# Four instead of two score products per step in the last attention's maxima stage

## The reference

```python
scores = jnp.einsum('bhtk,bhsk->bhts', q, k) * scale
weights = jax.nn.softmax(scores, axis=-1)
out = jnp.einsum('bhts,bhsk->bhtk', weights, v)
```

## Time and profile before

| | us |
|---|---|
| median of 3 runs | 3852.59 |
| lowest, highest | 3845.99, 3853.17 |
| profiled execution, whole | 3852.74 |
| its span, first to last instruction | 3851.0 |

### The profile page before, as it was taken

How to read it: one execution, slowest core, us unless ns; L and a number is a source line. 1 busy time by engine, 2 the same in 40 slices (tenths; PEclk the granted TensorE clock), 3 DMA queues, 4 the chain that set the end, 5 groups by cost and what they waited for, 6 DMA issues and landing times.

```text
span 3851.0 us, 43741 instructions
## 1 busy us (share of the span) xinstructions
PE 3115.1 (81%) x16174; PEld 1567.3 (41%) x16174; DVE 2426.6 (63%) x4576; ACT 1662.7 (43%) x2458; POOL 596.6 (15%) x425
## 2 busy tenths in 40 slices
PE   3647868997699868997699968998699977996698
PEld 1124423553245433554245532554235532464145
DVE  4634876568756776568765776668755786634442
ACT  3504625465255634465154644446154643432231
POOL 2001000311023010321013010321013110211030
PEclk8568969998799979998699989998799988997696
DMA  3151175302842165402843047412753128412261
GB/s 112 27 95 58 46 123 139 113 14 77 145 144 68 28 106 154 124 22 60 152 133 88 20 104 121 151 39 50 136 133 102 32 81 136 137 58 65 57 203 45
DMA packets 331910, 355.91 MB, mean 92 GB/s; under 512 B 98529, under 2 KB 264225, under 8 KB 330081
## 3 DMA queue, kind: packets, MB, share of 16 engines
q1 hardware_dynamic: 331697, 353.11, 39.1%
HBM read 302.74 MB, written 49.66 MB: 92 GB/s over the span
## 4 chain that ended last, share of the span: by engine, by line
PE 52%; DVE 28%; DMA 7%; ACT 5%; issue 4%; POOL 2%; SPq 2%; ACTq 0%; DVEq 0%; POOLq 0%
DVE MX L1596 7%; PE PS L1805 6%; PE PS L1828 6%; PE PS L1832 5%; PE PS L1659 5%; PE PS L1667 5%; PE PS L1103 3%; DVE U L891 3%; PE PS L1773 3%; DVE U L898 3%; DMA UU<-k_scratch 3%; PE PS L1784 2%; DVE D L1650 2%; POOL D L1404 1%; DVE D L948 1%
## 5 line engine op out<-in xcount | busy, mean ns | idle before, releaser
L1404 POOL TENSOR_TENSOR D<-D,GW 128x512 f32<-128x512 f32 x320 | 434.7, 1359 | 1409.1 <-ACT D L1477 1173.6
L783 ACT ACTIVATE U<-U 128x2048 f32<-128x2048 f32 x256 | 488.0, 1909 | 184.3 <-DVE U L891 99.4
L1645 DVE SCALAR_TENSOR_TENSOR D<-D,PS 128x512 f32<-128x512 f32 x336 | 229.2, 682 | 399.2 <-ACT D L1481 283.6
L1477 ACT ACTIVATE D<-PS 128x512 f32<-128x512 f32 x336 | 200.2, 596 | 610.2 <-PE PS L1828 610.2
L1805 PEld LDWEIGHTS PS<-WST,D 128*128 128x128 f32 (+1 forms) x2688 | 353.0, 198 | 163.4 <-DVE D L1650 96.0
L1805 PE MATMUL PS<-WST,D 128*128 128x128 f32 (+1 forms) x2688 | 380.3, 286 | 29.3 <-DVE D L1650 29.2
L1832 PE MATMUL PS<-XT,WST 128*128 128x512 f32 (+1 forms) x672 | 372.6, 637 | 29.2 <-DVE D L1645 28.0
L898 DVE SCALAR_TENSOR_TENSOR U<-PP,RD,QB 128x512 f32<-128x512 f32 x512 | 364.1, 780 | 47.5 <-ACT QB L780 28.8
L1103 PE MATMUL PS<-U,resident 128*32 128x512 f32 x2048 | 304.6, 675 | 102.3 <-ACT U L783 102.3
L1828 PE MATMUL PS<-XT,WST 128*128 128x512 f32 (+1 forms) x672 | 369.6, 633 | 7.7 <-DMA WST<-in_pairs_dram 4.7
L1596 DVE TENSOR_REDUCE MX<-PS 128x2 f32<-128x1024 f32 x256 | 298.4, 1221 | 84.9 <-PE PS L1751 84.9
(11 more groups left out here) (345 smaller groups left out, 3907.2 us busy)
## 6 DMA issues: line engine op xcount, KB each, us to landing
GW<-gates_scratch SPq DMA_DIRECT2D x320, 256.0 KB, 4.3
WST<-in_pairs_dram SPq DMA_DIRECT2D x336, 192.0 KB, 2.4
U<-band_scratch SPq DMA_DIRECT2D x32, 1280.0 KB, 14.6
UU<-in_w_dram SPq DMA_DIRECT2D x64, 512.0 KB, 7.6
UU<-pad_scratch SPq DMA_DIRECT2D x8, 1792.0 KB
UU<-q_scratch SPq DMA_DIRECT2D x24, 384.0 KB
UU<-k_scratch SPq DMA_DIRECT2D x24, 384.0 KB
e_scratch<-D SPq DMA_DIRECT2D x8, 1024.0 KB, 4.5
```

The source lines that it names most:

```text
L783: e.activation(ring(i), ring(i), ACT.Gelu).then_inc(S["act"], 1)
L1404: e.tensor_tensor(AV[:, n % 3, :], AV[:, n % 3, :], GW[:, p // 2 % GWS, p % 2, :], ALU.mult).then_inc(S["gated"], 1)
```

## The change

In each of the 32 steps PE issues four products in place of two. The first two are the same product into the same bank, and the third and fourth likewise; each starts a new accumulation, so the second overwrites what the first wrote. The semaphore is raised by the fourth. Nothing else differs: the waits, the reductions and the results are the same.

```diff
-                for x in range(2):
+                for x in (0, 0, 1, 1):
                     last = e.matmul(PZ(j + x), QS3[:, hd, P * (j + x):P * (j + x) + P], KS3[:, hd, :], start=True, stop=True)
                 last.then_inc(S["s1_3"], 1)
```

## The result

The changed kernel takes 3875.4 us (median of 4 runs, 3872.86 to 3883.8) against 3852.9 us of the kernel before; the ratio is 1.0066, with a 95% interval of 1.0046 to 1.0086. Run once more beside other kernels it gave 3883.6 us and a ratio of 1.0068 (1.0055 to 1.0081). It is slower, by some 25 to 26 us by the two ratios; the medians alone differ by 22.5 and 29.2 us. One execution of inner (4978.7 us) and one of halves (5201.1 us) further down ran at a mean granted clock of 0.592 and 0.549 against 0.87 to 0.91 in all others, and are left out of the ratios.

What follows compares the result with a forecast made beforehand. The maxima stage was taken to be on the chain, paced by DVE at full clock and PE's bank loop at low. Terms 6.7 + 8.0 + 3.6 + 15.2 - 2.0 = 31.5 us on 3852.7 gave 3884 us, range 3870 to 3900.

Steps and rivals of the forecast that it cites:

- The stage ends what both threads wait for: Maxima stage: L1154 and L1162 sit in PE's queue behind its last step, so both threads go on from its end.
- The price of a product: PE, start to start: 0.42 us at 1.2 GHz and 0.22 us at 2.4 GHz, taken for repeated products too.
- Term 1: Ahead of the first reduction: two more low-clock products, not hidden, 0.84 us a stage, 6.7 us in eight stages.
- Terms 2 and 5: Stage start: slow low-clock steps cost 1.0 us a stage, 8.0 in all; the clock's rise gives 2.0 us back once.
- Term 3: Steps at full clock: the pace stays 1.18 us and never gets to 1.13; together 3.6 us.
- Term 4: Around L1154: products added on either side cost 0.79 us at each of 3 x 7 places; 15.2 us after 1.4 back.
- What makes the stage longer makes the turn longer: Maxima stage: on the chain nearly whole, so its growth passes to the turn; summed in full, 31.5 us.
- Rival 1: Clock does not rise in the stage or falls back; 171 us more, 4024 us; chance 3%.
- Rival 2: Denser PE carries full clock beyond the stage and into its start, speeding L1162; 3860.5 us; chance 3%.
- Rival 3: Repeated product nearly free at the full clock; 6.8 us stay, 3859.5 us; chance 3%.
- Rival 4: Half of the delay covered by a transfer or engine that ends after the stage anyway; 3868 us; chance 7%.
- The allowance of 10 us for the clock: Over seven turns, 10 us either way for where the clock falls and rises against the work.

Runs made afterwards that it cites:

- inner: Against the kernel before, repeated products only in steps 4 to 21, 24, 25, 28 and 29, away from the stage's start and L1154; ratio 1.0025.
- halves: Kernel before with each L1154 in two halves of 8 products, one step of the maxima really between them; ratio 0.9954.
- split: Kernel before with L1154 meant to be in two parts, but nothing came between them, so the queue is as before; ratio 1.0003.
- again: The changed kernel run once more without an edit, for a second profile; 3883.6 us, ratio 1.0068 to the kernel before.
- six: Each product three times instead of twice as in the change, six a step; ratio 1.0226 to the kernel before.
- first4: Against the kernel before, repeated products only in the first four steps of the stage; ratio 1.0017.
- beside: Against the kernel before, repeated products only in the six steps right beside the three L1154; ratio 1.0017.
- three: Against the kernel before, three products a step away from L1154 and two beside it; ratio 0.9993.
- warm7: Kernel before with seven products nobody reads while PE waits for the stacks ahead of the stage; ratio 0.9993.
- warm7_four: The changed kernel with seven products nobody reads while PE waits for the stacks; ratio 1.0054 to the kernel before.

## Why the prediction was right, and where it was off

The direction was right and the time lies in the range: 3875.4 us measured, 3884 forecast. Step by step:

- The stage ends what both threads wait for: right. The six turns with both threads grew from 440.5 to (3215.7 - 548.6)/6 = 444.5 us, by 4.0, where the stages in them grew by 4.4 in the mean. With the second profile of either queue (split 441.3, again 444.7) the growth is 3.2 to 4.2. Only, the three L1154 of the earlier trace rows stand between steps of the stage, not behind its last one; no term depends on that.
- The price of a product, 0.42 and 0.22 us: right, and six shows it with the loop of 2.79 us.
- Term 1 (0.84 us): 1438.95 - 1437.03 = 1.92 us from first load to first reduction, against 1.07 before: 0.85.
- Terms 2 and 5 (1.0 - 0.25 us a stage): the clock rose 4.0 to 5.4 us after the start. In item 2 the second and third interval are 1.71 and 1.28 us against twice 1.18, 0.63 together; over all eight stages they cost 0.5 to 1.1. About as forecast.
- Term 3 (the pace stays 1.18): 2.17 + 0.19 us for two steps, right to the digit.
- Term 4 (0.79 us at 21 places): 0.97 - 0.20 = 0.77. Over all 21 places, with the longer intervals that items 0 and 3 had before, that is 14.8 us where 15.2 were forecast.
- Sum: 31.5 forecast, 30.7 to 32.5 us measured in the stages.
- The rest: this is the step that failed. "What makes the stage longer makes the turn longer" was taken one to one, and the medians show 22.5 us in the first comparison, 29.2 in the second, 24.3 by the means of 9 and 64 executions. The stages' 32 us thus reached the time for about three quarters to four fifths. In the other kernels the share is different: 87 of 96 us in six, nearly all in first4 and inner, a third in beside. Two things of this are shown. The base was low: 3852.6 us is the median of three executions, where 64 more have a mean of 3855.3. With that base the same sum gives 3886.8, 7 us above the mean of the nine executions, so part of how near the forecast came is luck. And the rest varies by itself: in thirteen of the fourteen profiles it lies between 2748.6 and 2763.3 us, with no order by the length of the stage. Among the kernels without added products ahead of the stage, the two with the shortest rest, beside and halves, are also those with the least low clock in it: 397 and 388 us, against 415 and 418 in the queue before and 424 and 428 in the change. That is a coincidence of one profile each and not a test. What is not shown is whether the rest shrinks when the stage grows, since each kernel has one profile and both of the change's are of longer executions than its mean. The allowance of 10 us for the clock covered it.
- Rival 1 is out (full clock for all but the first 4 to 5.4 us). Rival 2 is out as well: every stage of the change begins at the low clock, and L1162 never ran faster than 1057 ns in this profile. Its four products took 3.75 us in each of the seven turns, where before they had taken 1.96 us in item 0's turn and some 3.5 in five others; that is about 3 us lost, which the sum doesn't have. Rival 3 is out by six. Rival 4, the partial cover, is the one that the numbers leave room for; no run here shows what would do the covering.

On the two rules that were weighed: the figure of 131 ns for each product, from the Trainium skill's "TensorE: Matmul & The Clock Gate", section "Back-to-back issue gap", differs from the trace, which has 0.22 us at the full clock in the change, in six and in three. The prediction's estimate of some 10 us by that figure shows no working: with 0.131 us for each product repeated at the full clock, and all else as in rival 3, the sum is 6.8 + 21 x 4 x 0.131 = 17.8 us, an estimate too. The section "A second HAM failure mode: psum-queue depth-cycling" of the same page of the Trainium skill describes what warm7 may have met, where steps of two products with pauses lost a clock that had been full at their start. The change didn't meet it, and in first4 the same steps of two kept the full clock in all eight stages but for 0.7 us, so nothing here contradicts the small chance that it was given.

## What to carry to other kernels

Ask of each place where work is added which engine is waited for there, not how busy the engine is on the whole: one more product a step was free once the clock was full (three), two more cost little but the start and a lost gain in the pace (inner), and two more on either side cost their full length beside a block that already overran the step (beside). A block that overruns the slack of a pipelined loop is worth cutting in parts that fit, which here went with 0.46% (halves), of which the stages show two fifths. And a stage that is made shorter meets the next thing that was just in time, here the DMA of the band. Compare stages within the traces before believing a few microseconds of a whole kernel: one queue's executions differed by 12 us (the change) and 20 us (before).

## What was not expected of the hardware

One and the same pattern held either clock, and no run shows what decides between them. Steps of two products with PE's short pauses went on at 0.50 for 27.3 us in warm7, and for the whole last stage in before. The same steps stayed at 1.00 for 27.3 us in before, once the clock had come up late in the stage (item 2), and for 35.1 us in first4 behind four doubled steps. In warm7 seven stages began at 1.00 behind the pause for the stacks (1.68 us in item 3), and all fell to 0.50 within 2.2 us; it took 6.8 to 27.4 us until the clock was back. With the same seven products ahead and four a step (warm7_four) the clock fell in four of seven stages, within 1.0 us of the start, and was back after 3.4 to 3.5 us. With three a step from a low start (three) it was up after 3.9 to 5.6 us and stayed, in item 2 for 34 us. Where three, four or six products were issued in each step from the start on, the clock was up within 6 us of the start in every stage. Whether the pause ahead of the stage or the steps made it fall in warm7 was not tried apart.
